# The expert part on 46 flat tiles of 128 tokens in place of 48 tiles of 124, with new engine orders

## The reference

```python
h = tok(x, kernel, bias)            # 9-tap convolution, scaled by the window's norm, tanh, relu: (16, 367, 128)
h = h + attn(layernorm(h), ...)     # q, k, scores; softmax in bands of radius 12, 84 and 90; mean of the three; Wo; layernorm
h = h + ffn(layernorm(h), ...)

def ffn(hidden, Wq, bq, ln_g, ln_b, keys0, keys1, expert_down, expert_up):
    q = (hidden @ Wq.T + bq).reshape(b, s, 8, 64)                # 8 heads, layernormed per head
    s0 = l2norm(q[..., :32]) @ l2norm(keys0).T                   # 64 scores
    s1 = l2norm(q[..., 32:]) @ l2norm(keys1).T                   # 64 scores
    sc0, ix0 = top_k(s0, 16); sc1, ix1 = top_k(s1, 16)
    fs, pos = top_k(all 256 sums sc0 + sc1, 16)                  # expert number = ix0 + ix1
    w = softmax(fs)
    act = gelu(hidden . expert_down[fi])
    return sum over heads and k of act * w * expert_up[fi]
```

## Time and profile before

| | us |
|---|---|
| median of three runs | 1461.08 (1459.81 to 1461.68) |
| profiled execution, its own time | 1458.15 |
| its span, first to last instruction | 1456.3 |
| VectorE busy | 1332.5 (91%) |
| TensorE busy | 1219.2 (84%) |
| GpSimd busy | 975.1 (67%) |
| ScalarE busy | 894.5 (61%) |
| mean granted TensorE clock | 0.723 of full speed |

### The profile page before, as it was taken

One profiled execution on the slowest core, in us unless ns is written; L12 is line 12 of the kernel. 1 busy time (PEld: TensorE's weight loads), 2 busy tenths in 40 slices (PEclk: granted clock), 3 DMA queues, 4 the chain that ended last, 5 costly groups with the idle time before them and its releaser, 6 DMA issues.

```text
span 1456.3 us, 41234 instructions
## 1 busy us (share of the span) xinstructions
PE 1219.2 (84%) x9633; PEld 711.9 (49%) x9633; DVE 1332.5 (91%) x10235; ACT 894.5 (61%) x4105; POOL 975.1 (67%) x1850
## 2 busy tenths in 40 slices
PE   4788887898888988888887979898898889998873
PEld 2434554644554464545445445554645555463343
DVE  4349999999999999999999999999999999998995
ACT  2566757567576656757675775767567576655532
POOL 4428667686867668586766857577685867667562
PEclk7777687767777676877867786687668777675655
DMA  2000000000000000000000000000000000000000
GB/s 52 12 6 2 3 10 4 4 8 5 9 4 10 3 5 10 5 9 4 11 4 4 10 4 10 5 10 4 5 8 6 4 4 5 3 4 3 5 3 7
DMA packets 22351, 10.49 MB, mean 7 GB/s; under 512 B 13839, under 2 KB 21951, under 8 KB 22080
## 3 DMA queue, kind: packets, MB, share of 16 engines
q1 hardware_dynamic: 21456, 7.30, 2.1%
q10 hardware_dynamic: 624, 0.30, 0.1%
HBM read 4.58 MB, written 3.01 MB: 5 GB/s over the span
## 4 chain that ended last, share of the span: by engine, by line
DVE 35%; PE 28%; issue 15%; POOL 14%; ACT 7%; SPq 1%; POOLq 1%; DVEq 0%; DMA 0%; ACTq 0%
DVE idx L1404 8%; DVE val L1402 5%; DVE oh L1417 4%; DVE scores L1407 4%; DVE cr L1471 4%; PE bankS L1132 3%; PE bankS L1131 3%; PE bankQ L1121 3%; PE bankQ L1120 3%; DVE best L1469 3%; ACT ns_junk L829 3%; PE bankM L1168 3%; PE bankQ L1108 2%; POOL std L561 2%; DVE wl L1436 2%
## 5 line engine op out<-in xcount | busy, mean ns | idle before, releaser
L1404 DVE FIND_INDEX8 idx<-val,scores 124x8 uint16<-124x64 f32 x1536 | 304.8, 217 | 0.0
L1168 PE MATMUL bankM<-wl,oh 128*128 128x16 f16 x5952 | 163.7, 173 | 59.5 <-DVE wl L1436 59.5
L1402 DVE MAX8 val<-scores 124x8 f32<-124x64 f32 x1536 | 211.1, 209 | 2.1 <-ACT scores L836 2.0
L1168 PEld LDWEIGHTS bankM<-wl,oh 128*128 128x128 f16 x5952 | 161.2, 101 | 72.6 <-issue 41.1
L595 POOL TENSOR_TENSOR ce<-idxf 124x128 f32<-124x128 f32 (+4 forms) x240 | 95.4, 429 | 115.9 <-ACT idxf L843 115.8
L829 ACT ACTIVATE ns_junk<-bankQ 124x32 f32<-124x32 f32 x768 | 138.2, 265 | 37.7 <-PE bankQ L1121 37.7
L1417 DVE TENSOR_SCALAR oh<-eh 128x992 f16<-128x992 int16 x384 | 150.4, 457 | 2.3 <-ACT eh L877 2.3
L1407 DVE MATCH_REPLACE8 scores<-val,scores 124x64 f32<-124x64 f32 x768 | 151.7, 208 | 0.0
L569 POOL TENSOR_TENSOR qscale<-nmx,power 124x16 f32<-124x16 f32 x48 | 139.9, 2914 | 0.0
L829 ACT ACTIVATION_READ_ACCUMULATOR ns_junk<-bankQ 124x1 f32 x768 | 138.3, 278 | 0.0
L1132 PE MATMUL bankS<-bias9k,std9T 9*124 9x512 f32 x192 | 132.2, 774 | 0.0
(11 more groups left out here) (188 smaller groups left out, 3185.0 us busy)
## 6 DMA issues: line engine op xcount, KB each, us to landing
x_in<-in_x SPq DMA_DIRECT2D x16, 93.8 KB
x_in<-in_x SPq DMA_DIRECT2D x16, 62.5 KB
out<-o_sb SPq DMA_DIRECT2D x16, 62.0 KB
out<-o_sb SPq DMA_DIRECT2D x16, 61.0 KB
out<-o_sb SPq DMA_DIRECT2D x16, 60.5 KB
x_in<-in_x SPq DMA_DIRECT2D x16, 31.0 KB
conv_w<-in_L_tok_kernel ACTq DMA_DIRECT2D x2, 128.0 KB, 3.0
fwq_in<-in_L_ffn_Wq SPq DMA_DIRECT2D x1, 256.0 KB
```

What stands on the lines that cost most here:

```text
L1168: last = e.matmul(coef[:, g, :, :], oh[:, k, g, :, :].rearrange("p v t -> p (v t)"), wl[:, part, k, :, TG * g:TG * (g + 1)], start=k + par ...
L1402: last = v.max(out=v_[:, hd, s, best8], in_=src[:, hd, s, :])
L1404: last = v.max_index(out=i_[:, hd, s, best8], in_max=v_[:, hd, s, best8], in_values=src[:, hd, s, :])
```

## The change

1. The expert part no longer follows the three tiles of a batch. The 16 x 367 = 5872 rows are taken as one list and cut into 46 tiles (NQ) of 128 rows (QT), the last of 112. Batches 0 and 1 have two expert tiles each, batches 2 to 15 three each (`has`, `flat`, `count`). All expert buffers grow from 124 to 128 rows. The first part stays as it was, on tiles of 124.
2. A tile can hold rows of two batches. `hnT` becomes 624 columns wide (WIDE); `p1_hnT` writes the 367 columns of a batch behind what the batch before left over, and a new step `p1_carry` on ACT copies 240 columns, the left-over, into the other buffer first. DVE clears both buffers at its start.
3. The residual h is written to a DRAM tensor `h_rows` by three DMAs per batch (`keep`) and read back as tiles of 128 rows into `h_in` (`fetch`); `finish` reads `h_in` and waits for that load. The output is stored as 128 rows of the flat output. All of these go through SP. `p1_h` waits for `keep` of two batches before instead of for `finish`.
4. The order lists of all five engines are new.

```diff
+QT = 128
+NQ = -(-B * T // QT)
+LASTQ = B * T - (NQ - 1) * QT
+NG = QT // TG
+WIDE = 3 * QT + 240
...
+            def flat(self, t):
+                return 2 * self.b + t if isinstance(self.j, int) and self.b < 2 else 3 * self.b + t - 2
...
+            def keep(c):
+                b = c.b
+                sp.wait_ge(h_ready, 3 * (b + 1))
...
+                for t in range(3):
+                    f = FIRST[t]
+                    sp.dma_start(rows_of(h_rows, T * b + OFF[t] + f, NT - f), h[c.par][f:NT, t, :]).then_inc(kept, 16)
+            def fetch(c, t):
+                b, n = c.b, c.flat(t)
+                sp.wait_ge(kept, 48 * (b + 1))
...
+                wait(sp, out_ready, n - 2)
...
+                sp.dma_start(h_in[0:m, c.third(t), :], rows_of(h_rows, QT * n, m)).then_inc(h_back[c.third(t)], 16)
...
-                do(store, c + -2, 0)
-                do(store, c + -2, 1)
-                do(store, c + -2, 2)
+                each(fetch, c + -1, 0)
+                each(store, c + -2, 2)
+                do(keep, c)
+                each(fetch, c + -1, 1)
+                each(store, c + -1, 0)
+                each(fetch, c + -1, 2)
+                each(store, c + -1, 1)
...
-                wait(pool, out_ready, 3 * (b - 1))
+                wait(pool, kept, 48 * (b - 1))
+                wait(pool, hn_ready, b - 1)
...
+            def p1_carry(c):
+                b = c.b
+                act.wait_ge(hnT_ready, b + 1)
+                wait(act, scored, c.flat(0))
+                wait(act, inner_done, EL * b)
+                a.activation(hnT[1 - c.par][:, 0:240], hnT[c.par][:, c.count() * QT:c.count() * QT + 240], ACT.Copy).then_inc(carried, 1)
...
-                e.matmul(bankQ[:, 0:3 * NT], down_x[:, low, :, :].rearrange("p h t -> p (h t)"),
+                e.matmul(bankQ[:, 0:c.count() * QT], down_x[:, low, :, :].rearrange("p h t -> p (h t)"),
...
-                v.scalar_tensor_tensor(out=o_sb[:, t, :], in0=ffn, scalar=1.0 / WSCALE, in1=h[c.par][:, t, :], op0=ALU.mult, op1=ALU.add)\
+                dve.wait_ge(h_back[c.third(t)], 16 * (c.turn(t) + 1))
+                v.scalar_tensor_tensor(out=o_sb[:, c.third(t), :], in0=ffn, scalar=1.0 / WSCALE, in1=h_in[:, c.third(t), :], op0=ALU.mult, op1=ALU.add)\
...
+                v.memset(hnT[0][:, :], 0.0)
+                v.memset(hnT[1][:, :], 0.0).then_inc(padded, 1)
...
-                do(q_scale, c, 0)
...
+                each(q_scale, c, 0)
+                do(p1_sbias, c + 1, 0)
+                each(rank_sums, c + -1, 2, 2)
```

587 lines of the change are left out of this document (311 added, 276 removed).

## The result

The changed kernel takes 1467.47 us (median of 8 runs, 1464.73 to 1469.84), where the kernel before takes 1460.44 (8 runs). The ratio is 1.0067, 95% interval 1.0039 to 1.0094 (the two medians alone give 1.0048, inside the interval). It is slower by 0.7%, where 2% faster was forecast. The profiled execution took 1466.9 us with a span of 1465.0, so the two profiled executions differ by 8.7 us, as the medians do (7.0).

The account below looks back on a forecast made before the run. VectorE, 91% busy, was taken to set the stage, with PE's chain adding 1 to 4 us of waiting. The terms 6.8 - 25.5 - 12 + 1 = -29.7 us took 1461.08 to 1431 us, range 1407 to 1466.

Parts of the forecast that it names:

- The start: Before the first tanh: turn_weights ahead of the first convolution on PE delays everything behind it, +6.8 us (3 to 8).
- Two light stages: Stages 1 and 2, each with one tile fewer, fall to 72 us each: 25.5 us gained, at least 13, at most 49.
- Tiles of 128 rows: In each stage DVE's tables grow by 0.5 us, and PE's work by 1 to 1.5 us.
- p1_windows: Stages 3 to 14: POOL's long additions move away from DVE's tables, gaining 2.0 us a stage; low end nothing.
- Other reordering: DVE's moved steps could win or lose 2.4 us a stage; +0.5 us a stage taken, with PE's growth.
- rival B: Contention and waits only change places, DVE waiting for cs: stages 1.5 us longer, 1461 us; chance 0.17 including unshortened stages 1 and 2.
- sign of being wrong: Stages 3 to 14 at 86 us or longer, DVE waiting for cs or one_high beside a q_scale; or late h loads.
- The end: The stretch after the last stage: three more tiles of growth and a slow scatter, +1 us.
- Memory round trip: Three more stores and three more loads of the residual per batch on SP, taken as 0.
- q_scale: POOL's 2.9 us step, now first in its body, just before the second tile's tables: cost 0, bound 2.9 us.
- rival C: A late q_scale on POOL holds up one_high of the second tile, 3.9 us a stage: 1490 us; chance 0.13.
- Rival A: More comes free: light stages fall to 60 us (1407), or three-tile stages to 82.5 us (1414); chance 0.24.

Follow-up runs that it names:

- start_back: The changed kernel with turn_weights on PE and copy_weights on ACT back where they were before; 1461.23 us, 1.0015 of the kernel before.
- experiment 7: Idle matmul pair added on PE to raise its clock 29 to 39 us into a stage: 1.0113 on the changed kernel; on tiles_only too spread for a ratio.
- xT_behind: tiles_only with p1_windows early on POOL, p1_turn_x early on PE and ACT's p1_xT behind p1_probs(2); 1434.4 us, 0.9877 of the kernel before.
- windows_mid: xT_behind with POOL's p1_windows one step later, behind the second half of cs; 1435.38 us, 0.9829 of the kernel before.
- tiles_only: The changed kernel with the old order lists on PE, ACT, POOL and DVE, SP's list new; 1433.89 us, 0.9836 of the kernel before.
- pool_old: The changed kernel with POOL's list alone as before; 1476.97 us, 1.0137 of the kernel before.
- experiment 3: The changed kernel with DVE's order around the first tile's tables, DVE's whole list, or POOL's whole list as before; 1.0078, 1.0088 and 1.0137.
- mended: The changed kernel with turn_weights, copy_weights, low_weights(2), p1_wsq put back, ACT's p1_xT and index_floats(0) moved; 1452.13 us, 0.9955 of the kernel before.
- order_only: The kernel before, with its old tiles, and the new order lists on PE, ACT, POOL and DVE; 1480.4 us, 1.0162.
- actpe_new: tiles_only with ACT's and PE's lists as in the changed kernel; 1471.88 us, 1.0108 of the kernel before.
- dve_new: tiles_only with DVE's list alone as in the changed kernel; 1455.95 us, 0.9991 of the kernel before.

## Why the prediction was wrong

**The start** was right in its mechanism: tanh begins at 26.41 us instead of 19.80, the convolution takes 5.84, and the first `p1_res` comes 8.1 us later (6.8 taken, 3 to 8 the bounds). start_back got back 0.5%, and its first `p1_res` comes at 51.4. The new rows:

```profile
16.71 1.12 PE L1049 MATMUL bankS<-id,fwq_in 128*128 128x128 f32 x4 [8.92 <-DMA up_x<-in_L_ffn_expert_up]
17.62 0.42 PE L1051 MATMUL bankM<-id,down_in 128*128 128x128 f32 x1
17.83 5.84 PE L1094 MATMUL banks<-xT,conv_w 128*128 128x367 f32 x10
```

**Two light stages** were right: 73.8 us each for the 72 taken, 21.9 us gained for 25.5, and for the reason given, since DVE works 56.8 and 57.4 of 73.8 us and the chain sets the stage.

**Tiles of 128 rows**: the three tables went from 199.0 us in twelve stages to 203.3 with the new tiles alone, 0.36 us a stage for 0.5. What I didn't see: with the new tiles and the old lists the stages fall from 84.95 to 83.65 instead of rising by 1.0. The alternation of 83 and 87 us is gone; from stage 4 to 13 all stages lie between 83.3 and 83.7. The stages with a slow stretch (clock under 0.7 in experiment 7) are gone with it; why they are isn't shown. I had written stage 10's extra 4 us down to PE's work and left them in.

**`p1_windows`**: the mechanism and its size were right (1.8 us a stage on good lists), and on the good base it was worth nothing in time (xT_behind 0.9877, windows_mid 0.9829, tiles_only 0.9836). Among the other new lists POOL's saves 0.7%, by pool_old in experiment 3. In the changed kernel one_low fell from 35.9 to 27.0 us and one_high from 115.1 to 110.4, but low_weights rose from 48.0 to 54.6. At 494 us `select` on POOL, behind a ce that had waited 3.3 us for ACT's idxf, lies beside it, and both are stretched (the additions of `select` take 1.03 us when alone):

```profile
494.19 2.09 DVE L1524 TENSOR_TENSOR wl<-wm,ol 128x1024 f16<-128x1024 f16 x2
```

```profile
494.26 1.47 POOL L684 TENSOR_TENSOR wcell<-taken,ce 128x400 f16<-128x400 f32 x1 [0.98 <-DVE taken L1568]
```

The step that failed in general: the sum took DVE's working time for the stage's time, and bounded what the orders could lose by DVE's idle time ("DVE's remaining idle time, 84.9 - 82.5 = 2.4 us a stage, is what it could win; as much could be lost"). DVE did work 7.4 us less in the twelve stages, and the stages took 18.5 us more: its idle time grew by 25.9, most of it the wait for the first scores.

**Other reordering** is the term that was mis-sized, and the sign was lost with it. For all that the new lists do the sum had -2.0 for `p1_windows` and +0.5 for the rest, -1.5 us a stage; the runs put them at +2.8 (86.5 against 83.65), or some 2.3 if tiles_only is taken at its median. The tiles, for which the sum had +0.5, brought -1.3. Together that is +1.5 us a stage where -1.0 was forecast. Its upper bound, as much lost as there was idle, 2.4 us, had no mechanism behind it and was given no rival of its own. The prediction said "I can't price this row by row"; rival B had 1.5 us a stage, which is what the stages lost, but the wait that it named (best for cs) is 6.0 us in the twelve stages, a tenth of the idle time: that its number was near is luck. The prediction's own sign of being wrong, stages of 86 us with DVE waiting for cs, came true in its first half. The bounds of its terms don't give the span of 1415 to 1450 either: start 8, light stages -13, twelve stages at 0.5 + 0 + 2.4 and 1 for the end make +30.8, 1492, so by its own bounds 1467 was within reach. What remains open is which steps make the 86.0 us of mended; DVE's list, PE's, and ACT's with PE's each cost by themselves, and five visible delays put right gave 1.1%.

**The end**: +5.1, where the sum had +1; tiles_only has +4.5. In it DVE waits 3.7 us for the expert scores (L1490), in tiles_only 3.4, where the wait was 0.8 before. Why wasn't tested.

**Memory round trip and `q_scale`**: no wait of DVE is released by a DMA in stages 3 to 14. `q_scale(0)` starts 39 to 40 us into a stage, takes 2.9 us, and the tables begin at 44.5 or later: it lies on nothing, so rival C's 1490 had a mechanism that never came about. Three rows also speak against its premise that a GpSimd instruction holds VectorE however little data it reads: in order_only (743.42 and 1088.25 us) and actpe_new (1070.74) the `lnr` step of POOL, 0.86 us on three elements a row, is under way when one_low begins 0.05 to 0.32 us later, and the first instruction of one_low takes its usual 0.23 us. Beside `sq_pairs` of `p1_windows`, begun 0.15 us before it, it takes 0.73 (pool_old, actpe_new). Rival A's first half didn't come; its second half, 82.5 us a stage, nearly did, but with the old lists (83.65). That the total is slower has its reason in no rival of mine.

**What beats both**: the new tiles with the old lists, 0.9836 [0.9807, 0.9864]; windows_mid, 0.9829 [0.9783, 0.9875], can't be told from it.

## What to carry over

In a kernel whose limiting engine is 97% busy, the order lists of the engines are fitted to one another: price a new set of lists by the slowest chain and not by the engine's work, and allow it to lose more than the idle time that is left (tiles_only idles 1.2 us a stage, and the new lists took 2.3 to 2.8). Build a change of sizes and a change of orders apart; here one gave 1.6% and the other took 2.3%. Time taken off the busiest engine is a gain only if no other wait takes its place: look up the next one in the same stage, and the one behind it.

## What the runs showed of the hardware

- A GpSimd addition of 0.19 us is held for 2.6 to 2.9 us when it starts 0.06 us or less ahead of a run of eight VectorE table instructions (or four of them and two of low_weights), in 107 cases of 15 traces; 0.2 us ahead (one case) and from 0.49 us on it is free. It is held to the end of the run and not of one instruction.
- A GpSimd instruction of 0.86 us on three elements a row (`lnr`) didn't hold a VectorE table instruction begun 0.05 to 0.32 us behind it (0.23 us, three cases); one of 0.81 us on 373 elements did (0.73 instead of 0.22).
- Swapping two neighbouring VectorE steps of 0.16 and 0.31 us cost 1.0% of the kernel (ratio 0.9941 against 0.9836).
- The granted clock of PE in one 10 us stretch ranges from 0.50 to 0.88 from stage to stage of the same loop (windows_mid), and the stage from 87.1 to 82.5 us; which of the two follows the other isn't shown.
- Behind the loop's branch DVE's first instruction came up to 1.7 us late in some kernels and on time in others, the kernel before, tiles_only and dve_new among them, whatever DVE's own list was; POOL's came 2.9 to 3.2 us late in the kernel before and 0.8 to 1.0 in tiles_only, with the same list.
